# A sampled convolution's gathers written out with their indices read in place, one scan's carry copied by ScalarE, and the dense batches begun two turns earlier

## What is computed

```python
def step(h, xs):
    d_t, B_t, C_t, u_t = xs
    dA = jnp.exp(d_t[..., None] * A)
    h = dA * h + (d_t * u_t)[..., None] * B_t[:, None, :]
    y = jnp.einsum('bdn,bn->bd', h, C_t)
    return (h, y)
```

```python
val = w00 * gather(y0i, x0i) + w01 * gather(y0i, x1i) + w10 * gather(y1i, x0i) + w11 * gather(y1i, x1i)
val = val * msk
out = jnp.einsum('op,bphw->bohw', weight, col)
```

## Time and profile before

| | us |
|---|---|
| median of three runs | 999.51 |
| the profiled execution's own time | 1002.18 |
| its span, first instruction to last | 1000.3 |
| TensorE busy | 781.6 (78%) |
| VectorE busy | 839.6 (84%) |
| ScalarE busy | 375.3 (38%) |
| GpSimd busy | 579.2 (58%) |
| granted TensorE clock, mean | 0.837 |

### The profile page before, as it was taken

How to read it: one execution, slowest core, us unless ns; L and a number is a source line. 1 busy time by engine, 2 the same in 40 slices (tenths; PEclk the granted TensorE clock), 3 DMA queues, 4 the chain that set the end, 5 groups by cost and what they waited for, 6 DMA issues and landing times.

```text
span 1000.3 us, 8282 instructions
## 1 busy us (share of the span) xinstructions
PE 781.6 (78%) x2365; PEld 377.9 (38%) x2365; DVE 839.6 (84%) x1164; ACT 375.3 (38%) x535; POOL 579.2 (58%) x528
## 2 busy tenths in 40 slices
PE   2445878587778688678778787769379999999997
PEld 1122323132223134344444453424355444444443
DVE  3888854799999678699999999985989898989994
ACT  1120056655454135311111111101058587676640
POOL 0000000277664057777777777777777777777774
PEclk9676988799999698677677776776559999999998
DMA  5000018000000541111111112128352745444422
GB/s 123 0 0 1 0 32 170 4 0 1 0 1 0 116 95 47 49 51 53 50 50 50 50 50 53 48 72 205 93 150 82 198 134 146 119 138 121 124 66 53
DMA packets 32339, 69.82 MB, mean 70 GB/s; under 512 B 12368, under 2 KB 12624, under 8 KB 31184
## 3 DMA queue, kind: packets, MB, share of 16 engines
q1 hardware_dynamic: 16080, 35.27, 13.4%
q0 software_dynamic: 15360, 31.49, 12.1%
q10 hardware_dynamic: 864, 2.64, 1.2%
HBM read 54.94 MB, written 5.77 MB: 61 GB/s over the span
## 4 chain that ended last, share of the span: by engine, by line
PE 43%; DVE 24%; POOL 8%; issue 6%; ACT 2%; DMA 1%; DVEq 0%; ACTq 0%; SPq 0%; POOLq 0%
PE PS L1614 20%; POOL got L788 6%; PE PS L823 6%; DVE scratch L1307 5%; DVE scratch L1229 4%; PE PS L1167 3%; DVE scratch L1314 2%; PE PS L1631 2%; PE PS L1182 2%; DVE prodg L799 2%; PE PS L863 2%; PE PS L1407 2%; DVE PS L1226 2%; DVE prodg L803 1%; PE PS L976 1%
## 5 line engine op out<-in xcount | busy, mean ns | idle before, releaser
L788 POOL DMA_INDIRECT got<-corner_table,idx_slot x405 | 405.2, 1001 | 123.4 <-issue 122.8
L1167 PE MATMUL PS<-parts,selb 96*128 96x512 bf16 (+1 forms) x256 | 88.6, 447 | 83.3 <-DVE scratch L1229 41.9
L1182 PE MATMUL PS<-scratch,wt 128*128 128x512 f32 x256 | 147.5, 707 | 0.5 <-DVE scratch L1314 0.5
L1614 PE MATMUL PS<-scratch,UZ 128*128 128x512 f32 (+1 forms) x288 | 133.3, 612 | 2.9 <-DVE scratch L1599 2.9
L788 POOL DMA_INDIRECT got<-corner_table,idx_all x75 | 80.2, 1069 | 61.6 <-DVE prime L1481 39.0
L823 PE MATMUL PS<-ln_g,w 128*128 128x32 f32 x576 | 102.7, 346 | 0.0
L823 PEld LDWEIGHTS PS<-ln_g,w 128*128 128x128 f32 x576 | 100.0, 270 | 0.0
L829 ACT ACTIVATE G<-PS 128x32 f32 (+1 forms) x32 | 6.2, 195 | 227.9 <-PE PS L823 214.1
L1167 PEld LDWEIGHTS PS<-parts,selb 96*128 96x128 bf16 x256 | 23.3, 117 | 156.8 <-DVE scratch L1229 56.5
L1182 PEld LDWEIGHTS PS<-scratch,wt 128*128 128x128 f32 x256 | 59.6, 233 | 58.7 <-issue 49.7
L1591 ACT ACTIVATE scratch<-UZ,knot 128x512 f32<-128x512 f32 (+1 forms) x128 | 81.6, 708 | 0.4
(11 more groups left out here) (362 smaller groups left out, 1351.9 us busy)
## 6 DMA issues: line engine op xcount, KB each, us to landing
UZ<-dense_rows SPq DMA_DIRECT2D x24, 512.0 KB, 4.0
got<-corner_table,idx_slot POOLq DMA_INDIRECT x405
UZ<-dense_rows SPq DMA_DIRECT2D x96, 64.0 KB, 2.2
XN<-ln_g SPq DMA_DIRECT2D x6, 256.0 KB, 5.7
got<-corner_table,idx_all POOLq DMA_INDIRECT x75
corner_table<-scratch SPq DMA_DIRECT2D x1, 1056.0 KB
corner_table<-XN SPq DMA_DIRECT2D x1, 1056.0 KB
X<-in_x SPq DMA_DIRECT2D x4, 256.0 KB
```

Of the source, the lines that this page charges most:

```text
L788: pool.indirect_dma_start(got[:, slot, tap, :, :].rearrange("p k c -> p (k c)"), None, tables[b], bass.IndirectOffsetOnAxis(ap=index[:, ta ...
L1167: last = nc.tensor.matmul(PS[:, first + n, :], selb[:, which, j, :], parts[:, bass.ds(i * CHUNK + n * BANK, BANK)], start=True, stop=True)
L1182: last = nc.tensor.matmul(PS[:, 4 + n, :], wt[:, W_SUM:W_SUM + P], dBC[:, j % 2, n * BANK:(n + 1) * BANK], start=False, stop=(j == PAIRS - 1))
L1614: last = nc.tensor.matmul(PS[:, n % 4, :], steps[rows, j, :, :].rearrange("p b c -> p (b c)"), ramps[k][rows, j, :], start=(j == 0), stop= ...
```

## The change

It does five things. GpSimd's gathers of all groups are written out and read `idx_all`; `idx_slot`, its copies by VectorE and the padding of `idx_all` go, and GpSimd waits for the second half of an image's indices ahead of the image's group 16. In image 1's scan the copy into `carry` moves from VectorE to ScalarE, behind the exponential and the turn of the same step; it waits for the scan (`h_done`) and signals `carried`, for which VectorE waits ahead of the next scan, since `hs` is one buffer. A further priming memset gives that signal its first count. The dense batches begin behind turn 27 instead of 29, and are spread from there to turn 62. The store of image 0's result moves from batch 5's place to batch 7's.

```diff
--- before.py
+++ after.py
@@ -706,7 +706,7 @@
         pr = {n: sem("proj_" + n) for n in ("xc_psum", "z_psum", "u_done", "z_done", "dt_psum", "v_ready", "bc_psum",
                                             "hi_done", "r_read", "clamp_done", "exp_done", "log_done", "mid_done", "parts_ready", "delta_ready")}
         sc = {n: sem("scan_" + n) for n in ("b_psum", "c_psum", "b_used", "exp_done", "h_done", "hc_done", "y_done", "y_used",
-                                            "dbu_done", "du_done",
+                                            "dbu_done", "du_done", "carried",
                                             "o_psum")}
         l3 = {n: sem("l3_" + n) for n in (
             "stats", "totals", "sqrt_go", "sqrt_done", "g_ready", "corner_ready", "right_ready", "shift_done", "below_in", "below_ready", "table_in",
@@ -725,8 +725,7 @@
                 for t in (chunk_buffer(0, 8), XN[:, :, :].rearrange("p b n -> p (b n)"))]
         temps = [XN[:, 0, :], scratch]
         tables = [nc.dram_tensor(f"corner_table_{b}", (L, 4 * C), F32, kind="Internal").ap() for b in range(B)]
-        idx_all = sb("idx_all", [P, (B * GROUPS + SLOTS) * TAPS], U32)
-        idx_slot = sb("idx_slot", [P, SLOTS, TAPS], U32)
+        idx_all = sb("idx_all", [P, B * GROUPS * TAPS], U32)
         coef = sb("coef", [P, B * GROUPS, TAPS, 4])
         got = sb("got", [P, SLOTS, TAPS, 4, C])
         got_flat = got[:, :, :, :, :].rearrange("p s t k c -> p (s t k c)")
@@ -793,7 +792,6 @@
 
             v.wait_ge(gathered[slot], arrived)
             v.nop(nofuse=True)
-            nc.vector.tensor_copy(idx_slot[:, slot, :], idx_all[:, bass.ds((G + SLOTS) * TAPS, TAPS)])
             if not isinstance(G, int) or G:
                 v.wait_ge(l3["col_done"], G)
             tell(v, nc.vector.tensor_tensor(prodg[:, 0:n, :, :].rearrange("p t k c -> p (t k) c"),
@@ -840,8 +838,6 @@
 
             n, m, slot = NEAR, (G - GROUPS) // 2, G % SLOTS
             v.wait_ge(gathered[slot], landed(G))
-            if G + SLOTS < B * GROUPS:
-                nc.vector.tensor_copy(idx_slot[:, slot, :], idx_all[:, (G + SLOTS) * TAPS:(G + SLOTS + 1) * TAPS])
             v.wait_ge(l3["col_done"], G)
             tell(v, nc.vector.tensor_tensor(prodg[:, 0:n, :, :].rearrange("p t k c -> p (t k) c"),
                                             got[:, slot, 0:n, :, :].rearrange("p t k c -> p (t k) c"),
@@ -1208,6 +1204,9 @@
                                      scale=negA[:, j:j + 1]).then_inc(sc["exp_done"], 1)
                 if j in TURN_AFTER:
                     between(TURN_AFTER.index(j))
+                act.wait_ge(sc["h_done"], s + 3)
+                act.nop(nofuse=True)
+                nc.scalar.activation(carry[:, j:j + 1], hs[:, CHUNK - 1:CHUNK], ACT.Copy).then_inc(sc["carried"], 1)
 
         def gate(v, tok, c):
 
@@ -1226,9 +1225,9 @@
                 tell(v, nc.vector.tensor_tensor(banks(0, 2), du, banks(0, 2), ALU.mult), sc["b_used"], s + 2)
                 v.wait_ge(sc["exp_done"], s + 1)
                 v.wait_ge(sc["hc_done"], s + 1)
+                v.wait_ge(sc["carried"], s - (LAST - 1))
                 tell(v, nc.vector.tensor_tensor_scan(hs, dA[:, j % 2, :], banks(0, 2), carry[:, j:j + 1], ALU.mult, ALU.add),
                      sc["h_done"], s + 3)
-                nc.vector.tensor_copy(carry[:, j:j + 1], hs[:, CHUNK - 1:CHUNK])
                 v.wait_ge(sc["c_psum"], s + 1)
                 v.wait_ge(sc["y_done"], s + 1)
                 nc.vector.tensor_tensor(dBC[:, j % 2, :], hs, banks(2, 2), ALU.mult).then_inc(sc["hc_done"], 1)
@@ -1647,7 +1646,7 @@
                 sp.dma_start(out[b].rearrange("c y x -> c (y x)")[:, q * QUARTER + 32 * first:q * QUARTER + 32 * last],
                              resids[b][32 * q:32 * q + 32, 32 * first:32 * last]).then_inc(l3["out_dma"], 16)
 
-        FIRST_TURN, LAST_TURN = 29, 62
+        FIRST_TURN, LAST_TURN = 27, 62
 
         def batches_after(G):
             return [n for n in range(len(BATCHES)) if FIRST_TURN + n * (LAST_TURN - FIRST_TURN) // len(BATCHES) == G]
@@ -1680,7 +1679,7 @@
                     prep[b][0](sp)
                 dense_first(sp)
                 for n in range(len(BATCHES) + 1):
-                    if n == 5:
+                    if n == 7:
                         store(sp, 0, 0, GROUPS)
                     if n < len(BATCHES):
                         dense_load(sp, n)
@@ -1711,15 +1710,10 @@
                     first = b * GROUPS
                     pool.wait_ge(l3["table_in"], 32 * (b + 1))
                     pool.wait_ge(l3["idx_ready"], 2 * b + 1)
-                    for G in range(first, first + SLOTS):
+                    for G in range(first, first + GROUPS):
+                        if G == first + GROUPS // 2:
+                            pool.wait_ge(l3["idx_ready"], 2 * b + 2)
                         group_gather(pool, b, G, G % SLOTS, idx_all[:, G * TAPS:(G + 1) * TAPS])
-                    turns = GROUPS // SLOTS - 1
-                    with nc.gpsimd.Fori(0, turns) as i:
-                        for k in range(SLOTS):
-                            slot = (first + k) % SLOTS
-                            group_gather(pool, b, i * SLOTS + (first + SLOTS + k), slot, idx_slot[:, slot, :])
-                    for G in range(first + SLOTS * (turns + 1), first + GROUPS):
-                        group_gather(pool, b, G, G % SLOTS, idx_slot[:, G % SLOTS, :])
 
             @block.tensor
             def _(pe):
@@ -1782,10 +1776,9 @@
             @block.vector
             def _(v):
                 norm_vector(v)
-                nc.vector.memset(idx_all[:, GROUPS * TAPS:], 0)
                 for k, (signal, n) in enumerate((
                         (sc["h_done"], 2), (sc["hc_done"], 1), (sc["y_done"], 2), (sc["y_used"], 1), (sc["b_used"], 1),
-                        (sc["dbu_done"], 2),
+                        (sc["dbu_done"], 2), (sc["carried"], 1),
                         (l3["prod_done"], SLOTS), (l3["o_psum"], SLOTS), (l3["o_read"], 2))):
                     nc.vector.memset(prime[:, k:k + 1], 0.0).then_inc(signal, n)
                 vchain(v, nc.vector.memset(carry[:, :], 0.0))
```

## The result

The changed kernel takes 1004.44 us in the median of seven runs (1003.50 to 1007.83), the kernel before 1000.20 in seven (999.06 to 1002.54). The ratio is 1.0040, with a 95% interval of 1.0025 to 1.0055: 0.4% slower, small but clear of noise, where I had predicted 997.5 and a range up to 1003.0. The profiled execution of the changed kernel took 1005.14 us, 0.7 above its median, that of before 1002.18, 2.0 above its own; so the traces show 3.0 us of the 4.2 between the medians.

The account below looks back on a forecast made before the run. GpSimd's gather chain and TensorE were taken to end within 0.1 us of each other, with GpSimd deciding. Terms -2.6, +1.0 and -0.1 gave -1.7 us, from 999.51 to about 997.8, stated as 997.5; range 991.5 to 1003.

Parts of the forecast that it names:

- what bounds the kernel: Whole kernel: GpSimd's gathers are a second, hidden chain, full end to end, ending within 0.1 us of TensorE's.
- more than 3.05: End of the kernel, a sign to look for: TensorE idle ahead of its last pair for more than 3.05 us.
- Rival 1: Dense stage: TensorE is the bound and GpSimd follows, so the time falls by 9 us to 990.5; chance 0.09.
- the gathers written out cost nothing: GpSimd's gathers, both images: the loop and index tile cost nothing, so writing gathers out changes the time by 0.
- Rival 4: Image 1's scan: ScalarE's copy and exponential do not fit into 2.51 us; time stays near 998; chance 0.06.
- rival 2: Dense stage: TensorE loses its clock, 2.8 us per slump; with seven slumps the end is 10.6 us later, 1010; chance 0.08.
- the scan: End of image 1's scan: VectorE 2.9 us earlier, from dropped index copies (1.6) and the carry copy on ScalarE (1.3).
- -2.6 us of lengthening: Gathers during image 1's scan: turns that come sooner hold gathers less over 20 turns, -2.6 us, bounds +0.6 and -5.
- +1 for 32 turns, bounds -2 and +3: Dense stage: VectorE overtakes the gathers, and waiting turns hold the next gather by their second product, +1 us.
- Rival 3: VectorE's turns: index copies hold gathers themselves, so removing them saves 4.7 us more, giving 992.8; chance 0.12.
- TensorE ends 9 us sooner: TensorE's chain: dense batches 11.0 us sooner plus the scan's 2.9, minus 4.8 for moved multiplications, about 9 us sooner.
- -1.7 us of span: Whole span: sum of -2.6 in the scan, +1.0 in the dense stage and -0.1 for the last turn's start.

Follow-up runs that it names:

- idx_allpad: Kernel before with gathers written out and indices read in place, but one idle index copy in every turn of both images; ratio 0.9988, median 999.87 us.
- carry_only: Kernel before with only the carry of image 1's scan copied by ScalarE instead of VectorE; ratio 1.0005 to before, median 1001.58 us.
- idx_only: Kernel before with only the index part changed: gathers written out, no `idx_slot`, no index copies by VectorE; ratio 1.0052 to before, median 1005.36 us.
- pad2_last60: Changed kernel with two idle copies ahead of the product in image 1's turns and the last dense batch behind turn 58; ratio 0.9994 to before, median 999.61 us.
- after_pad1: Changed kernel with one idle copy that nobody reads put into each turn of image 1; ratio 0.9976 to before, median 998.75 us.
- before_cut: Kernel before with two instead of six gathers for each of groups 62 and 63, eight fewer; ratio 0.9985 to before, median 1000.08 us.
- after_pad2: Changed kernel with two idle copies that nobody reads ahead of the product in each turn of image 1; ratio 0.9944 to before, median 996.53 us.
- after: The changed kernel with all parts of the change, against the kernel before; ratio 1.0040, median 1004.44 us.
- after_cut: Changed kernel with two instead of six gathers for each of groups 62 and 63, eight fewer; ratio 1.0017 to before, median 1003.22 us.

## Why the prediction was wrong, step by step

**Right: what bounds the kernel.** GpSimd's gathers are a chain from end to end, 0.30 us and 0.945 us each, without other waits. The last turn starts by the landing of the last gather, and TensorE idles 6.07 us ahead of its last pair (more than 3.05, as forecast). Rival 1 falls: the end did not follow TensorE.

**Right: the gathers written out cost nothing.** `idx_allpad` is within 0.15% of before. The carry copy is no cost either: `carry_only` is at 1.0005, VectorE never waits for the copy, ScalarE's 32 copies take 0.20 us each, the exponential follows behind (the kernel after, ScalarE):

```profile
427.93 0.20 ACT L1209 ACTIVATE carry<-scratch 128x1 f32<-128x1 f32 x1 [8.00 <-DVE scratch L1229]
428.04 1.13 ACT L1203 ACTIVATE scratch<-XN,negA 128x1024 f32 x1
```

Rival 4 falls with it, and rival 2 too: the granted clock of the dense stage is 0.97, and no slump sets the end.

**Not shown either way: the scan.** I had VectorE 2.9 us sooner at its end. In the traces turn 23 starts at 645.12, before at 655.44, 10.3 us; in `idx_only` at 646.78, in `carry_only` at 651.12. The first lines of turn 23, kernel before, kernel after, and `pad2_last60`, whose scan has the same code as that of the kernel after:

```profile
655.37 0.30 DVE L796 COPY idx_slot<-idx_all 128x9 uint32 x1
655.44 1.35 DVE L799 TENSOR_TENSOR prodg<-got,coef 128x1152 f32<-128x1152 f32 x1
```

```profile
645.12 1.35 DVE L797 TENSOR_TENSOR prodg<-got,coef 128x1152 f32<-128x1152 f32 x1
646.51 0.76 DVE L801 TENSOR_TENSOR prodg<-prodg 128x576 f32<-128x576 f32 x1
```

```profile
650.57 1.35 DVE L798 TENSOR_TENSOR prodg<-got,coef 128x1152 f32<-128x1152 f32 x1
```

Executions of the same scan differ by nearly as much. From the first scan instruction of image 1 to turn 23 it is 228.9 us in the kernel after, but 236.8 in `after_pad1` and 237.1 in `pad2_last60`; with the scan of before it is 238.6, in `before_cut` 233.3. In the two long executions of the changed scan VectorE waits for TensorE ahead of the product with C 7.5 and 8.0 us, in that of the kernel after 2.7, and before 7.5. So these waits come and go between executions of one scan, and much of the 10.3 us with them; what makes them was not tried. The means, 232.1 us over six and 236.6 over three, leave room for my 2.9 without proving it. The -2.6 us of lengthening that I forecast there is not borne out: -1.1 in the two traces, and over the same nine executions 8.4 us with the changed scan against 8.3 with the old one.

**The step that failed: "+1 for 32 turns, bounds -2 and +3"**, the lengthening in the dense stage. It measured +5.0. I had priced the effect of a turn that overtakes the gathers, and laid it to the earlier batches. Instead it is the removed copy of 0.08 us; overtaking alone holds little, since `after_pad2` waits for gathers in the dense stage 10 times, 25.9 us, with 7.4 us of lengthening. I had used exactly this argument for image 0 (a turn d sooner holds d less, down to nothing) and had not asked what it does where nothing is held: 8.75 us of a batch and a turn against 7 x 1.25 = 8.75 of gathers can be read from the earlier trace rows and the timeline, and 0.08 us less leaves it. A second copy does not (turns 44 to 46 of `after_pad2` are 8.74 and 8.73 apart). The cause is shown by taking the copies out and putting them back. The three kernels without a copy in image 1's turns and with the adds kept (`after`, `after_cut`, `idx_only`) have 12.9 to 14.0 us of lengthening, the ten with one or two 6.1 to 10.7; and `idx_allpad` and `after_pad1` take the time back (0.9988 and 0.9976 against 1.0052 and 1.0040) with the copies alone. Rival 3 had the copies as a cost to gathers; they are a benefit, so it fell with the wrong sign.

**The premise that failed: TensorE ends 9 us sooner.** TensorE in the kernel after, its first dense batch:

```profile
717.09 9.67 PE L1613 MATMUL PS<-scratch,UZ 128*128 128x512 f32 x18 [2.93 <-DVE scratch L1598]
```

It began even sooner than I said (717.09, forecast 726, before 739.66 in the earlier trace rows); that much was this execution's short scan, since in `after_pad1` it begins at 726.74. It ended where it had. Batches are tied to turns, the last one to turn 60 in both kernels; turns wait for gathers; so TensorE's lead is given back in VectorE's waits (36.5 us in the dense stage, 13.1 before) and its own 11.9 us of pauses. With the gathers of the last two groups mostly gone it had 2 us in hand. This premise did not enter the sum, since GpSimd's chain was the term, but it made rival 2 too mild and made the early batches look free of effect.

**The sum**, with the terms of the two traces: start +0.27, projection -1.2, scan -1.1, preparation -0.45, image 1 +5.0, tail +0.6: +3.1 us of span (3.0 by the page), against -1.7 predicted. Of these only image 1's term is far outside what executions of one kernel differ by.

## What to carry to other kernels

Where two engines share a lock and both run periodically, look at the ratio of their periods: near a whole number every repetition can meet the same phase, and removing work may cost more than it saves: here 0.08 us less on VectorE cost GpSimd some 0.35 us, in nearly each turn. Before an instruction is removed from an engine that does not end last, ask which engine's collisions it times; if the trace shows long runs of unlengthened instructions beside operations that lengthen others, that order is worth something and easily lost. Here two idle copies per turn put it back and made the fastest kernel of the study, 0.9944 (0.9922 to 0.9966) of before.

## What the runs showed of the hardware that was not expected

- A gather that asks within some 0.16 us of the start of a product or an add on two SBUF tiles is not held; asking 0.14 us after it, the add is 0.04 us longer instead (0.60 against 0.56). Asking 0.21 us after it, the gather is held by 0.36.
- A sum over four strided values per output by one reduction costs 1.51 us for 768 inputs per partition and 2.13 for 1152, against 0.92 and 1.22 for two adds.
- The same 18 multiplications of a group take TensorE 4.03 us in one place and 2.17 in another of the kernel after, where the granted clock is 0.50 (710 to 714 us) and 1.00 (727 to 729 us), the 1.2 and the 2.4 GHz level. Ahead of the slow one TensorE had been idle for 14.98 us, ahead of the fast one it had just run a dense batch:

```profile
710.13 4.03 PE L821 MATMUL PS<-ln_g,w 128*128 128x32 f32 x18
...
726.93 2.17 PE L821 MATMUL PS<-ln_g,w 128*128 128x32 f32 x18
```
